# Cross stage: the scores of two heads over 64 rows each, and ScalarE's copy of the inverse after the ramp

## The reference

```
scores = einsum(Q, K) / sqrt(32); scores = where(mask, scores, -inf)
topv, topi = top_k(scores, 32);  probs = softmax(topv)
attn = zeros.at[topi].set(probs);  attn_mean = attn.mean(over heads)
c_t = attn_mean @ (ctx Wv)
x = layernorm(x) * (1 + gate*scale_in(c_t)) + gate*shift_in(c_t)
y = irfft(rfft(x) * rfft(K_s4d)) + x * D_skip      # a long convolution along the tokens
```

## Time and profile before

| | |
|---|---|
| median of 3 runs | 5045.92 us |
| profiled execution | 5042.79 us |
| its span | 5040.9 us |
| granted TensorE clock, mean over the span | 0.855 |
| busy: TensorE, VectorE, ScalarE, GpSimd | 88%, 75%, 41%, 43% |

### The profile page before, as it was taken

One profiled execution on the slowest core, in us unless ns is written; L12 is line 12 of the kernel. 1 busy time (PEld: TensorE's weight loads), 2 busy tenths in 40 slices (PEclk: granted clock), 3 DMA queues, 4 the chain that ended last, 5 costly groups with the idle time before them and its releaser, 6 DMA issues. The chain is left out here.

```text
span 5040.9 us, 70529 instructions
## 1 busy us (share of the span) xinstructions
PE 4416.3 (88%) x28066; PEld 3194.9 (63%) x28066; DVE 3805.5 (75%) x4097; ACT 2068.8 (41%) x3816; POOL 2186.9 (43%) x2260
## 2 busy tenths in 40 slices
PE   8999977589999999999999999987579989898984
PEld 6777753356665676676766667667456666666662
DVE  5666659699999988888788887876256767777667
ACT  3433322144444444444444444431234545444453
POOL 1111116435454566766667666670233333333321
PEclk9999988678888877777777777788789999999996
DMA  2111115300011001111011110023531211111101
GB/s 84 51 46 50 49 48 185 118 24 28 24 42 61 26 28 34 38 53 36 28 32 38 54 37 26 30 69 76 193 104 43 61 44 58 47 58 54 51 26 36
DMA packets 214587, 275.98 MB, mean 55 GB/s; under 512 B 96659, under 2 KB 144403, under 8 KB 210224
## 3 DMA queue, kind: packets, MB, share of 16 engines
q1 hardware_dynamic: 196850, 216.91, 14.2%
q0 software_dynamic: 17408, 54.56, 2.9%
HBM read 186.44 MB, written 84.98 MB: 54 GB/s over the span
## 5 line engine op out<-in xcount | busy, mean ns | idle before, releaser
L1555 POOL TENSOR_TENSOR c_s<-c_s,c_z 128x2048 f32<-128x2048 f32 x128 | 580.5, 4535 | 792.8 <-ACT c_z L1344 790.8
L1875 PE MATMUL f_p_g<-f_hT,f_w 128*128 128x128 f32 x4096 | 538.3, 295 | 69.8 <-ACT f_gT L1975 55.4
L1496 DVE MAX8 c_top<-c_z 128x8 f32<-128x2048 f32 x256 | 585.0, 2285 | 4.7 <-issue 0.2
L1875 PEld LDWEIGHTS f_p_g<-f_hT,f_w 128*128 128x128 f32 x4096 | 526.7, 211 | 90.4 <-ACT f_gT L1975 58.2
L1497 DVE MATCH_REPLACE8 c_z<-c_top,c_z 128x2048 f32<-128x2048 f32 x256 | 582.6, 2276 | 0.0
L1169 PE MATMUL c_p_s<-c_kt,c_qT 32*128 32x512 f32 x1024 | 500.9, 864 | 87.1 <-ACT c_s L1334 85.8
L1179 PEld LDWEIGHTS c_p_a<-c_diag,c_s 128*128 128x128 f32 x4096 | 528.2, 211 | 49.5 <-ACT c_diag L1358 25.8
L1179 PE MATMUL c_p_a<-c_diag,c_s 128*128 128x128 f32 x4096 | 531.3, 293 | 25.2 <-ACT c_diag L1358 25.2
L1883 PE MATMUL f_p_o<-f_w,f_gT 128*128 128x512 f32 x1024 | 481.8, 592 | 0.0
L1334 ACT ACTIVATE c_s<-c_p_s 128x512 f32<-128x512 f32 x512 | 278.2, 594 | 455.0 <-PE c_p_s L1170 454.6
L1249 PE MATMUL c_p_m<-c_wf,c_uT 128*128 128x512 f32 x768 | 415.7, 684 | 22.6 <-ACT c_yb L1398 16.3
(11 more groups left out here) (362 smaller groups left out, 8103.4 us busy)
## 6 DMA issues: line engine op xcount, KB each, us to landing
mod_out<-c_fo POOLq DMA_DIRECT2D x32, 512.0 KB, 3.0
f_mr<-mod_out SPq DMA_DIRECT2D x32, 512.0 KB, 4.8
p_ct<-in_ctxT SPq DMA_DIRECT2D x16, 768.0 KB, 5.1
c_vals<-in_ctx SPq DMA_DIRECT2D x4, 3072.0 KB, 12.0
c_kb<-kspec SPq DMA_DIRECT2D x22, 512.0 KB, 3.3
a_xt<-in_xT SPq DMA_DIRECT2D x32, 256.0 KB, 3.1
a_xr<-in_x SPq DMA_DIRECT2D x32, 256.0 KB, 2.6
x<-a_out POOLq DMA_DIRECT2D x32, 256.0 KB, 2.5
```

Of the source, the lines that this page charges most:

```text
L1496: st.link(v.max(best[n], work))
L1555: pool.tensor_tensor(row, row, low, ALU.subtract).then_inc(cut_ready, 1)
L1875: last = mm(p_g[:, f % 8, :], w1[:, k, f * P:(f + 1) * P], hT[:, k * P:(k + 1) * P], start=(k == 0 and f % 4 == 0), stop=(k == KD - 1 and ...
```

## The change

The queries of a tile are no longer kept in two buffers for two tiles. They are copied twice, once per parity of the head, each time scaled by a column `hm` of ones and zeros, so that copy p holds heads p and 2 + p and zeros in the rows of the other two. A score matmul now takes 64 rows (heads 2i and 2i + 1, one of them zero in the queries) in place of 32, from rows 0 and 64. The pair p is now the heads p and p + 2; as each lands in the same place of the ring of rows as before, the order of the heads within a tile changes, and their mean does not. The mask rows are loaded at two partitions instead of four. In ScalarE's order, `copy_slot(t)` moves from before `below(j + 2)` to after it.

```diff
+            for h in range(NH2):                                   # VectorE, at the start
+                v.memset(hm[HS * h:HS * h + HS, h % 2:h % 2 + 1], 1.0).then_inc(hm_ready, 1)
+                v.memset(hm[HS * h:HS * h + HS, 1 - h % 2:2 - h % 2], 0.0).then_inc(hm_ready, 1)
...
-                for h in range(NH2):
-                    sp.dma_start(mrow[HS * h:HS * h + 1, :], mask_row[b:b + 1, :]).then_inc(keys_in, 16)
+                for r in (0, 2 * HS):
+                    sp.dma_start(mrow[r:r + 1, :], mask_row[b:b + 1, :]).then_inc(keys_in, 16)
...
-                pe.wait_ge(keys_in, 80 * (t // CH + 1))
+                pe.wait_ge(keys_in, 48 * (t // CH + 1))
...
-                        r = HS * (2 * p + i)
+                        r = 2 * HS * i
                         at_least(pe, s_copied, (t * 2 + p) * 8 + 2 * c + i - 1)
-                        mm(p_s[:, i, :], qT[r:r + HS, t % 2, :], kt[r:r + HS, cols], start=True, stop=False)
+                        mm(p_s[:, i, :], qT[r:r + 2 * HS, p, :], kt[r:r + 2 * HS, cols], start=True, stop=False)
                         mm(p_s[:, i, :], oneb[r:r + 1, :], mrow[r:r + 1, cols], start=False, stop=True).then_inc(s_done, 1)
...
-                a(qT[:, t % 2, :], p_m[:, 1, 0:P], ACT.Copy).then_inc(q_copied, 1)
+                for p in range(2):
+                    last = a(qT[:, p, :], p_m[:, 1, 0:P], ACT.Copy, scale=hm[:, p:p + 1])
+                last.then_inc(q_copied, 1)
...
+            act.wait_ge(hm_ready, 2 * NH2)
             copy_q(0)
...
-                if slot_job(t) is not None:
-                    copy_slot(t)
-
                 below(j + 2)
+                if slot_job(t) is not None:
+                    copy_slot(t)
```

More of the change, by code:

```diff
@@ L918, in cross @@
         tb = m.sb("tb", [P, 2])
+        hm = m.sb("hm", [P, 2])
         den = m.sb("den", [P, 2])
@@ L963, in cross @@
         p_m = m.ps("p_m", [P, 2, 512])
-        (core_in, film_in, consts, keys_in, values_in, s_done, s_copied, z_done, nb_ready, tb_ready, low_ready, cut_ready,
+        (core_in, film_in, consts, hm_ready, keys_in, values_in, s_done, s_copied, z_done, nb_ready, tb_ready, low_ready, cut_ready,
          sum_done, rd_ready, w_ready, im_ready, diag_ready, attn_done, aT_copied, uT_done, uT_copied,
@@ L971, in cross @@
             m.sem(n) for n in (
-                "core_in film_in consts keys_in values_in s_done s_copied z_done nb_ready tb_ready low_ready cut_ready "
+                "core_in film_in consts hm_ready keys_in values_in s_done s_copied z_done nb_ready tb_ready low_ready cut_ready "
                 "sum_done rd_ready w_ready im_ready diag_ready attn_done aT_copied uT_done uT_copied "
@@ L1433, in _ @@
                     copy_s(t + 1, 0, 1)
+                below(j + 2)
                 if slot_job(t) is not None:
                     copy_slot(t)
-                below(j + 2)
                 if t:
```

## The result

The changed kernel takes 5441.13 us, the median of 4 runs (5430.55 to 5445.77), against 5047.09 for the kernel before (5042.34 to 5048.26): the ratio is 1.078, with a 95% interval from 1.0761 to 1.0798. The profiled execution took 5444.72 us (span 5442.8). The time moved up by 394 us; 5433 was forecast.

What follows compares the result with a forecast made beforehand. TensorE, slowed by its clock (0.78), was taken to bound the cross stage, with VectorE's floor near 66 us a tile. 64 scores phases at 6.1 us more added 390 to 5042.8, other terms 0: 5433 us, range 4860 to 5490.

Steps and rivals of the forecast that it cites:

- all four rivals: Other outcomes: overlap, clock held, 4890; one head at a time, clock held, 4930; other head passes switch, 5210; nothing, 5043.
- What a switch costs, and which matmuls make one: Scores phases: one-row masks between 64-row scores make four switches a chunk, about 0.2 us each with hold-up.
- One head at a time: Scores phases: the queue holds at each switch, so the two heads no longer overlap; forecast case, chance 0.51.
- The price of a head: Scores chunk: two passes, mask and two switches take 1.47 us at full clock, 2.51 at half.
- The clock: Scores phases: TensorE's clock falls about 5 us in, as before, making a phase about 16.3 us instead of 10.2.
- The sum: Cross stage: 64 scores phases at 6.1 us more each give 390 us, on 5042.8: 5433.
- The query copy, the mask rows, the memsets: One more ScalarE copy a tile (0.277 us), fewer mask transfers, eight small memsets: each taken as 0.
- The copy behind the ramp: Cross tiles: VectorE regains some 7 us a tile, TensorE nothing; 0 where TensorE bounds, pays only if TensorE gets faster.
- the first: Scores phases: heads still overlap and the clock holds; at most -200 us, middle 4890; chance 0.28.
- The second rival: Scores phases: one head at a time but the clock holds; phase 11.6 us, total 4930; chance 0.07.
- the third: Scores phases: the queue lets the other head pass the switch; chunks 2.65 and 3.7 us, total 5210; chance 0.09.
- The two ends of the range: Total time: 4860, toward heads overlapping with clock held, and 5490, toward one head at a time with clock falling.

Runs made afterwards that it cites:

- the four copies first: 64-row scores and masks, split order, plus ScalarE copying all four chunks of a phase before weighing: 4885.89 us; with slot's copy ahead of the ramp everywhere, 4839.72 us.
- a kernel that was run later: Changed kernel with both heads' scores, then both one-row masks, in each chunk, two switches in place of four: 5172.05 us, ratio 1.0243.
- masks together: Changed kernel with TensorE's order in a chunk altered to both heads' 64-row scores, then both one-row masks: 5172.05 us, ratio 1.0243.
- split order: Changed kernel with 64-row masks and ScalarE's copy behind the ramp only in 21 tiles with an inverse, ahead in eight with short transposes: 4941.23 us, ratio 0.9793.

## Why the prediction was right

The mechanism was right, and 5433 stands against 5441. That the time lies in the range says less: it went from 4860 to 5490 and held the times of all four rivals. Part of the nearness is luck, as the sizes show. Taken by its own steps:

- *What a switch costs, and which matmuls make one.* Right. The gaps of 0.093 and 0.13 us in the earlier trace rows were read as the price of a change of height. In the changed kernel the second pass of the second head starts at 2496.72 (2496.19+1.12-0.59) and the mask at 2497.25, some 0.52 us later, where a pass alone takes 0.427: 0.1 more. The switch back costs 0.31 (2495.88 to 2496.19) less 0.213, 0.1 again. That the array is empty in between is not to be seen in the rows; they show that nothing passes, and these 0.1 us.
- *One head at a time.* Right, and shown: overlap is lost with the one-row mask, back with the 64-row mask, and back within each kind when the program puts like heights together.
- *The price of a head.* 1.47 us were worked out at full clock and 1.37 measured; 2.51 and 2.53 at half. The term that was too large is the hold-up of 0.1 us behind the switch to the mask: there is one only behind the switch to the scores (0.53 us from first to second pass).
- *The clock.* Right that it falls in every phase; that the length of the phase came out to the tenth of a microsecond is luck. The fall was taken to come 5 us into the phase; over 62 phases it came 3.7 to 5.6 us in, 4.7 in the mean (5.3 in the phase shown). The earlier fall costs about what the cheaper head saves: 4.7 us make 1.7 chunks of 2.74, the other 2.3 take 11.6 us at 5.07, and that is the 16.3 us that were forecast from 5 us, 2.9 and 5.0. Measured are 16.3 in the mean, 15.6 to 17.0.
- *The sum.* The starts of matmuls in the two traces give 668.3 us in all 64 scores phases before and 1050.4 after, 382 more; 390 were forecast. The profiled executions lie 402 us apart, so some 20 us stand outside the phases, where the sum had nothing, the waits of 1.84 us in the tiles with transposes among them. Too much by 8 and too little by 20 is why the total is near.
- *The query copy, the mask rows, the memsets*: 0 was taken. A scaled copy takes 0.36 us (L1329, 64 of them), and not the 0.28 of a plain one that was put in. Once, ahead of the first scores, an instruction of TensorE waits for it; otherwise nothing of these three is seen in the tiles, but none was run by itself.
- *The copy behind the ramp.* Right that it gives nothing in the late tiles; wrong that it costs nothing. The step looked at a tile with an inverse of 7.1 us, under which the ramp is hidden, and carried that to the eight tiles with 1.1 us of transposes, where it is not. The price was a wait of 1.84 us, and alone, with the clock, 25 us of the whole. Wrong too, that it pays once TensorE gets faster: with 64-row masks its place is worth nothing clear of noise, and with the four copies first it costs 1%.

Of the rivals, the first (overlap kept, clock held) gave 4890; it is what happens once the cause against it is taken away: 4926 with the mask at 64 rows, 4886 and 4840 with the copies in a better order. Its doubt about ScalarE's weighing was right: the clock fell in that hole or the chunk behind it in 31 of 62 phases, and without the hole it held in 59. The second rival is excluded by the clock in the trace, the third by the order of the heads, though it named the times of a kernel that was run later.

The two ends of the range lay 630 us apart, and one reading decided between them: whether the one-row mask is of the same kind as 32 rows and not as 64.

## What to carry to other kernels

Before changing the height of a matmul's tile, list the heights of all matmuls that stand between: an odd one of a single row cost about 0.3 us around it here (1.37 us a head, of which 1.07 are two passes and a mask) and, much more, the overlap of tiles that run side by side. Give all of them the same height (rows of zeros cost nothing here), or put like heights together in the program. When the clock falls in a stretch of small tiles, look at how many rows are in use there and at the holes in it; both mattered here, 64 rows for the scores and masks of each head and the copies ahead of the other work.

## What the hardware showed beyond this

The places of the clock's fall in the 62 scores phases behind the first tile's two, counted from each phase's start, tell more than one phase does:

| kernel | phases with a fall | us into the phase, mean (range) |
|---|---|---|
| before: 32-row scores, one-row masks, two at a time | 62 | 4.5 (3.6 to 5.8) |
| changed: 64-row scores, one-row masks, one at a time | 62 | 4.7 (3.7 to 5.6) |
| masks together: 64-row scores two at a time, one-row masks | 62 | 4.7 (4.2 to 7.1) |
| 64-row scores and masks, two at a time | 39 | 6.9 (4.5 to 9.7) |
| the same, split order, four copies first | 3 | 5.0 (4.9 to 5.0) |

- Rows that are zero in one operand count as use. With 64-row scores and masks the clock held longer than with 32-row scores and one-row masks at the same start times and lengths (0.90 against 0.78 over the late tiles; 4926 against 5070 us for the two kernels with the same order of copies). Half of the query rows are zeros, while the keys that meet them are not, and 63 of the 64 mask rows are zeros.
- The height of the scores alone does not hold it. With the masks together two 64-row score matmuls stand side by side too, the masks have one row and a chunk is 2.62 us instead of 2.08, and the clock fell in every phase. How much of the gain is the rows of the mask and how much the shorter chunk was not separated.
- Denser is not enough. TensorE had no hole in the phases of the changed kernel, with one 64-row tile at a time, and its clock fell as early as with two 32-row tiles and holes.
- A wait of 1.83 us moved half-clock stretches elsewhere in the tile: eight tiles, 25 us.
